# Selections, logits, one-hot transposes and scatters in another order on TensorE

## The chip, the core and the metric

The kernel runs on one core of a Trainium2 chip. The metric is the device time of one execution in microseconds (us); the median of several executions is compared. TensorE (PE) multiplies, VectorE (DVE) and ScalarE (ACT) copy and compute, GpSimd (POOL) helps, and SyncE (SP) issues most transfers. Engines run side by side and meet at semaphores; each works through its own instructions in the order in which they are written.

## The reference

```python
def _L0_gnn_ref(h, adj, Wq, bq, Wk, bk, Wv, bv, Wo, bo):   # masked attention, 8 heads
    ...
    scores = jnp.einsum('bhqd,bhkd->bhqk', q, k) * scale
    attn = jax.nn.softmax(jnp.where(mask, -jnp.inf, scores), axis=-1)
    ...
def _L0_ffn_ref(x, controller, f1, f2):                     # 64 expert slots, groups of t=16 tokens
    cont_logits = jnp.einsum('bgtd,des->bgtes', grouped, controller) + tie
    cont_perm = (cont_logits == jnp.max(cont_logits, axis=-3, keepdims=True)).astype(x.dtype)
    intermediate = jnp.einsum('bgtd,desf->bgtesf', grouped, f1)
    inner = jax.nn.relu(jnp.einsum('bgtesf,bgtes->bgesf', intermediate, cont_perm))
    inter2 = jnp.einsum('bgesf,esfd->bgesd', inner, f2)
    result = jnp.einsum('bgesd,bgtes->bgtd', inter2, cont_perm)
x = x + _L0_gnn_ref(_layernorm(x), ...)
x = x + _L0_ffn_ref(_layernorm(x), ...)
```

x is 32 x 256 x 256 in float32. In each group of 16 tokens every one of the 64 expert slots picks the token with the highest logit; the pick is a one-hot row. The second half of the kernel, which the change touches, selects those tokens, runs the experts on them and adds the results back to the tokens' rows.

## The kernel before

The 8192 token rows are 64 tiles of 128. The attention goes over 32 batches and fills the first two thirds of the span. The expert part goes over 4 chunks (c) of 16 tiles; a chunk is 4 units (u) of 4 tiles, and n = 4c + u counts the units from 0 to 15. After the four units of a chunk comes `experts(c)`.

What TensorE does in a unit (L909 to L931), each with the engine that takes the result:

- `unit_transpose(n + 2)` (L700) transposes the normalised tokens of the unit after next into banks 0 and 1; ScalarE copies them (`save_h2T`, L971).
- `select(n, t)` for t = 0 to 3 (L798) multiplies tokens by one-hots. A selection has two halves: the first goes to a bank pair that VectorE copies, the second to one that ScalarE copies (`copy_selected`, L284). The halves of t = 0 to 3 rotate over bank pairs 4, 6 and 0, so a half waits for the copy of the half three before it (L807 to L815): the second half of the fourth selection waits for VectorE's copy of the third.
- `one_hot_transpose(n + 1)` (L721) transposes the next unit's one-hots into bank 2; ScalarE copies them to `permR` (`save_one_hot`, L977).
- `logits(n + 2)` (L708) also writes bank 2, so it waits for that copy (`perm_saved`). On VectorE follow `tied_logits` (L1300), `group_maximum` (L1307) and `one_hot` (L1312).
- `scatter(c - 1, s)` (L895), two of them in each of the last three units of chunks 1 to 3, adds back the results of the chunk before: pair s is tiles 2s and 2s + 1, both into bank 3, and VectorE adds the bank to the tokens (`finish`, L1444). A scatter waits for the finish before it and, half by half, for its tile's results to have landed in SBUF (`gathered`, L902). Pairs 6 and 7 stand in `experts(c)` (L942).

The results of the experts go through HBM, since they are made by expert and needed by group. During `experts(c)` SyncE writes 16 blocks to `scratch` (`move`, L433). Then it gathers the 16 tiles, each in two halves (`gather`, L441), into a ring of 5 slots: tiles 0 to 4 follow each other as soon as the blocks are written, tile i from 5 on waits until tile i - 5 was scattered (L444). SyncE issues in order: first halves of tiles 0 to 3, then the second half of tile 0, of tile 1, and so on (L464 to L472).

In chunk 0 there are no scatters. There VectorE also does small steps of a reciprocal square root (`late_root_steps`, L1440) in unit 0 from t = 2 on, in units 1 and 2 and at the start of unit 3. In unit 0 it finishes the last attention batch as well. Units 14 and 15 have no unit transpose and no logits; unit 15 has no one-hot transpose.

Of the kernel before, what the change touches and what calls it, by code (L numbers as in the profile page):

```python
# [23 lines left out]
def gnn_moe_kernel(nc, x, adj, Wq, bq, Wk, bk, Wv, bv, Wo, bo, controller, f1, f2, out):  # L24
    B, N, D = x.shape
# [10 lines left out]
    CT = 16  # L36
    CHUNKS = TILES // CT
    UT = 4
    UNITS = CT // UT
# [9 lines left out]
    AHEAD = 2  # L49
# [24 lines left out]
    with ExitStack() as ctx:  # L74
# [88 lines left out]
        bank = [banks[:, i, :] for i in range(8)]  # L163
# [43 lines left out]
        res_done = sem("res_done")  # L207
# [380 lines left out]
        def _(pe):  # L588
# [101 lines left out]
            def o_project(b, last=False):  # L690
                pe.wait_ge(onorm_done, b + 1)
                if not last:
                    pe.wait_ge(q_saved, b + 3)
                for t in range(QT):
                    for g in range(G):
                        done = nc.tensor.matmul(M[1][:, t * D:t * D + D], OT[:, g, t * P:t * P + P], WT[:, 3, g, :],  # L696
                                                start=(g == 0), stop=(g == G - 1))
                done.then_inc(wo_ready, 1)
# [9 lines left out]
            def logits(n, into=bank[2]):  # L708

                pe.wait_ge(h2T_saved, n + 1)  # L710
                if n > 0:
                    pe.wait_ge(perm_saved, n)
                for k in range(KT):
                    for half in range(2):
                        r = slice(64 * half, 64 * half + 64)
                        own = h2T[:, k, :].rearrange("p (c two t) -> p c two t", two=2, t=T)[:, :, half, :]
                        last = nc.tensor.matmul(into[r, 0:UT * P // 2], ctl[:, k, :], own,  # L717
                                                start=(k == 0), stop=(k == KT - 1))
                last.then_inc(log_ready, 1)

            def one_hot_transpose(n, into=bank[2]):  # L721
                pe.wait_ge(perm_done, n + 1)
                for t in range(UT):
                    last = nc.tensor.transpose(into[:, t * P:t * P + P],
                                               permT[region(n)][:, t * P:t * P + P], ident[:, :])
                last.then_inc(pbt_ready, 1)
# [71 lines left out]
            def select(n, t):  # L798
                tile = n * UT + t
                if t == 0:  # L800
                    pe.wait_ge(perm_saved, n + 1)
                if tile == 0:
                    pe.wait_ge(perm_done, AHEAD)
                if t == 0 and n > 0 and n % UNITS == 0:
                    pe.wait_ge(st_dve, n // UNITS * QUADS)
                    pe.wait_ge(st_act, n // UNITS * QUADS)
                for hf in range(2):  # L807
                    if t == 0 and n > 0:
                        pe.wait_ge((sel_dve, sel_act)[hf], tile)
                    elif (t, hf) == (1, 0) and n + AHEAD < CHUNKS * UNITS:  # L810
                        pe.wait_ge(h2T_saved, n + AHEAD + 1)
                    elif (t, hf) == (1, 0):
                        pe.wait_ge(sel_act, tile - 2)
                    elif t > 0:
                        pe.wait_ge((sel_act, sel_dve)[hf], tile - 1 + hf)  # L815
                    for k in range(KT):
                        for j in (2 * hf, 2 * hf + 1):
                            r = slice(32 * j, 32 * j + 32)
                            last = nc.tensor.matmul(bank[pair_of(t, hf) + j % 2][:, k * P:k * P + P], h2[n % NORMS][r, t, k * P:k * P + P],  # L819
                                                    permR[r, n % 2, t * P:t * P + P], start=True, stop=True)  # L820
                    last.then_inc((sel_low, sel_ready)[hf], 1)
# [73 lines left out]
            def scatter(c, s):  # L895

                n = c * (CT // 2) + s
                if n > 0:
                    pe.wait_ge(fin_done, n)
                for tt in range(2):  # L900
                    tile = 2 * s + tt
                    pe.wait_ge(gathered[tile_slot(c, tile)], arrived(c, tile))  # L902
                    for j in range(4):
                        last = nc.tensor.matmul(bank[3][32 * j:32 * j + 32, tt * D:tt * D + D],  # L904
                                                chosen(c * CT + tile, j), XR[:, tile_slot(c, tile), j, :],
                                                start=True, stop=True)
                    last.then_inc(sc_ready, 1)

            def unit(c, u):  # L909

                n = c * UNITS + u
                ahead = n + AHEAD < CHUNKS * UNITS
                pairs = scatters(u) if c > 0 else ()
                if ahead:
                    if n > 0:
                        pe.wait_ge(sel_act, n * UT - 1)
                    unit_transpose(n + AHEAD)
                select(n, 0)
                if n + 1 < CHUNKS * UNITS:
                    one_hot_transpose(n + 1)  # L920
                if n == 0:
                    o_project(B - 1, True)
                select(n, 1)
                if ahead:
                    logits(n + AHEAD)
                select(n, 2)
                if pairs:
                    scatter(c - 1, pairs[0])
                select(n, 3)
                if pairs:  # L930
                    scatter(c - 1, pairs[1])  # L931

            def experts(c):
                pe.wait_ge(sel_dve, (c + 1) * CT)
                pe.wait_ge(sel_act, (c + 1) * CT)
                if c == 0:
                    pe.wait_ge(ffn_in, 16 * 2)
                expand(c, 0)
                for w in range(TWOS):
                    if w + 1 < TWOS:  # L940
                        expand(c, w + 1)
                    if c > 0 and w < len(LATE):  # L942
                        scatter(c - 1, LATE[w])
                    contract(c, w)

# [12 lines left out]
        def _(act):  # L958
# [18 lines left out]
            def save_one_hot(n, src=bank[2]):  # L977
                act.wait_ge(pbt_ready, n + 1)
                nc.scalar.copy(permR[:, n % 2, :], src[:, :]).then_inc(perm_saved, 1)
# [115 lines left out]
            def save_selected(c, u, t):  # L1095
                act.wait_ge(sel_ready, c * CT + u * UT + t + 1)
                copy_selected(nc.scalar.copy, c, u * UT + t, 1).then_inc(sel_act, 1)

            def unit(c, u):
                n = c * UNITS + u  # L1100
                ahead = n + AHEAD < CHUNKS * UNITS
                if ahead:
                    save_h2T(n + AHEAD)
                save_selected(c, u, 0)
                if n + 1 < CHUNKS * UNITS:
                    save_one_hot(n + 1)
                save_selected(c, u, 1)
                save_selected(c, u, 2)
                save_selected(c, u, 3)

            def experts(c):
# [25 lines left out]
        def _(dve):  # L1137
# [298 lines left out]
            def save_selected(c, u, t):  # L1436
                dve.wait_ge(sel_low, c * CT + u * UT + t + 1)
                copy_selected(nc.vector.tensor_copy, c, u * UT + t, 0).then_inc(sel_dve, 1)

            def late_root_steps(c, u, t):  # L1440
                if c == 0 and 2 <= u * UT + t < ROOT_STEPS + 2:
                    roots_step(u * UT + t - 2, slice((B - 4) * QT, TILES), late_root)
# [15 lines left out]
            def unit(c, u):  # L1458
                n = c * UNITS + u
                ahead = n + AHEAD < CHUNKS * UNITS  # L1460
                pairs = scatters(u) if c > 0 else ()
                save_selected(c, u, 0)
                late_root_steps(c, u, 0)
                save_selected(c, u, 1)
                if n == 0:
                    last_result()
                late_root_steps(c, u, 1)
                if ahead:
                    tied_logits(n + AHEAD)
                save_selected(c, u, 2)  # L1470
                late_root_steps(c, u, 2)
                if ahead:
                    group_maximum()
                if pairs:
                    finish(c - 1, pairs[0])
                save_selected(c, u, 3)
                late_root_steps(c, u, 3)
                if pairs:
                    finish(c - 1, pairs[1])
                if ahead:  # L1480
                    one_hot(n + AHEAD)
# [57 lines left out]
```

## Time and profile before

| | |
|---|---|
| median of 3 runs | 752.02 us (750.18 to 753.73) |
| the profiled execution, its own time | 753.89 us |
| its span, first to last instruction | 752.0 us |
| mean granted TensorE clock | 0.988 |
| PE busy, share of the span | 711.2 us, 95% |
| DVE, ACT, POOL busy | 79%, 72%, 24% |
| chain that ended last: PE | 86% |
| chain: waits on the gathers (DMA stage<-scratch) | 2% |

The page has the busy time of each engine, the span in 40 slices, the chain of work that ended last followed back from the end, and the costliest groups. In a row of the timeline stand the start and the duration in us, the engine, the line of the kernel, the operation, the tile written and the tile read, the shape and the count of merged instructions; in square brackets the idle time of that engine before it, and what ended it. PEld is the loading of TensorE's weights, which overlaps the multiplication; a matmul shows here as two instructions, a transpose as one. SPq is SyncE issuing a transfer. The granted clock is given as a share of the full 2.4 GHz, so that 0.5 is 1.2 GHz.

### The profile page before, as it was taken

How to read it: one execution, taken by the hardware profiler on the slowest of the kernel's cores; microseconds unless marked ns; L12 is line 12 of the kernel's file. 1: busy time of each engine (PE TensorE's matmuls, PEld its weight loads, DVE VectorE, ACT ScalarE, POOL GpSimd, SP SyncE). 2: the span in 40 equal slices, each digit the busy share in tenths (PEclk: the TensorE clock that was granted, in tenths of full speed). 3: DMA queues.
4: the chain of work that ended last, by engine and by line, in shares of the span. 5: the costliest groups of instructions: out<-in, count | busy, mean ns of one | idle time of the engine just before them, and what ended most of it. 6: DMA issues, size and time to landing. Idle time of an engine off the chain costs nothing.

```text
span 752.0 us, 22953 instructions
## 1 busy us (share of the span) xinstructions
PE 711.2 (95%) x7420; PEld 575.8 (77%) x7420; DVE 595.7 (79%) x2418; ACT 544.2 (72%) x1606; POOL 181.2 (24%) x375
## 2 busy tenths in 40 slices
PE   8899999999999999999999999989879979878888
PEld 7788888888888888888888888866656656655666
DVE  6698898898988988989889888986656756656566
ACT  4788989898889898988899889874445344344243
POOL 2130321302303213023032130646705506400000
PEclk9999999999999999999999999998999999999999
DMA  6776787677867877778678767746099798798943
GB/s 179 185 184 143 185 196 163 166 187 166 193 147 177 194 164 167 185 168 193 150 174 194 166 144 157 158 87 218 3 394 300 261 388 276 265 383 271 342 164 104
DMA packets 110742, 149.24 MB, mean 198 GB/s; under 512 B 14784, under 2 KB 75712, under 8 KB 110432
## 3 DMA queue, kind: packets, MB, share of 16 engines
q1 hardware_dynamic: 107904, 146.26, 72.0%
q10 hardware_dynamic: 2592, 1.71, 1.0%
q8 instruction: 37, 0.61, 0.3%
q0 software_dynamic: 192, 0.52, 0.2%
q14 instruction: 17, 0.14, 0.1%
HBM read 39.39 MB, written 33.55 MB: 97 GB/s over the span
## 4 chain that ended last, share of the span: by engine, by line
PE 86%; DVE 6%; issue 3%; DMA 2%; ACT 2%; SPq 1%; POOL 0%; DVEq 0%; POOLq 0%
PE bank L672 15%; PE bank L624 15%; PE bank L659 8%; PE bank L685 8%; PE bank L696 8%; PE bank L646 7%; PE bank L819 5%; PE bank L861 3%; DVE stage L1503 3%; PE bank L904 3%; DMA stage<-scratch 2%; PE bank L717 2%; PE bank L877 2%; PE bank L617 2%; PE bank L704 2%
## 5 line engine op out<-in xcount | busy, mean ns | idle before, releaser
L1026 ACT ACTIVATE Ps<-Ps,nmax 128x256 f32<-128x256 f32 x512 | 254.6, 501 | 19.8 <-DVE nmax L1246 19.8
L1246 DVE CUSTOM_DVE_ANT_0 Ps<-bank,masks 128x256 f32<-128x256 f32 x512 | 193.0, 421 | 28.6 <-issue 28.4
L672 PE MATMUL bank<-ident,Ps 128*128 128x128 f32 x1024 | 134.8, 274 | 2.5 <-ACT Ps L1026 1.8
L672 PEld LDWEIGHTS bank<-ident,Ps 128*128 128x128 f32 x1024 | 114.8, 141 | 11.9 <-issue 3.3
L624 PE MATMUL bank<-hT,WT 128*128 128x256 f32 x512 | 121.1, 380 | 0.3 <-ACT hT L983 0.3
L624 PEld LDWEIGHTS bank<-hT,WT 128*128 128x128 f32 x512 | 92.4, 190 | 10.7 <-ACT Vs L999 0.7
L549 POOL TENSOR_SCALAR h<-X,mv,roots 128x256 f32<-128x256 f32 x64 | 79.6, 1255 | 78.7 <-PE bank L819 76.5
L1026 ACT ACTIVATION_READ_ACCUMULATOR Ps<-Ps,nmax 128x1 f32 x512 | 97.4, 190 | 0.0
L659 PE MATMUL bank<-stack 128*128 128x256 f32 x512 | 91.5, 311 | 0.6 <-DMA stack<-parts 0.6
L1257 DVE COPY PTs<-bank 128x512 f32<-128x512 f32 x128 | 86.7, 677 | 0.2
L659 PEld LDWEIGHTS bank<-stack 128*128 128x128 f32 x512 | 71.7, 189 | 17.3 <-issue 13.1
L1035 ACT COPY PTs<-bank 128x512 f32<-128x512 f32 x128 | 73.5, 574 | 11.5 <-PE bank L672 11.5
L508 POOL TENSOR_TENSOR spread<-rsum,nans 128x128 f32<-128x128 f32 x32 | 12.9, 405 | 232.9 <-DVE rsum L1263 232.9
L1009 ACT ACTIVATE parts<-bank,few 128x256 fp32r<-128x256 f32 x128 | 53.0, 464 | 21.3 <-PE bank L624 21.3
L685 PE MATMUL bank<-PTs,Vs 128*32 128x256 f32 x1024 | 61.9, 382 | 0.8 <-DVE PTs L1257 0.8
L696 PE MATMUL bank<-WT,OT 128*128 128x256 f32 x256 | 62.3, 386 | 0.2
L646 PE MATMUL bank<-WT,hT 128*128 128x256 f32 x256 | 62.1, 387 | 0.0
L1120 ACT COPY stage<-bank 128x512 f32<-128x512 f32 x48 | 25.8, 589 | 49.6 <-PE bank L861 49.6
L819 PE MATMUL bank<-permR,h 32*128 32x128 f32 x1024 | 55.5, 303 | 5.5 <-DVE XS L292 3.2
L819 PEld LDWEIGHTS bank<-permR,h 32*128 32x128 f32 x1024 | 43.0, 192 | 23.0 <-issue 10.3
L1232 DVE SCALAR_TENSOR_TENSOR parts<-bank,few,parts 128x256 fp32r<-128x256 f32 x128 | 55.8, 479 | 1.9 <-ACT parts L1009 1.9
L292 ACT COPY XS<-bank 128x512 f32<-128x512 f32 x48 | 28.3, 589 | 32.7 <-PE bank L819 31.8
(107 smaller groups left out, 1052.9 us busy)
## 6 DMA issues: line engine op xcount, KB each, us to landing
stack<-parts SPq DMA_DIRECT2D x506, 128.0 KB, 2.5
scratch<-stage SPq DMA_DIRECT2D x48, 512.0 KB, 4.3
stage<-scratch SPq DMA_DIRECT2D x96, 256.0 KB, 4.4
X<-in_x SPq DMA_DIRECT2D x32, 256.0 KB, 2.9
out<-X SPq DMA_DIRECT2D x32, 256.0 KB, 3.7
rbc<-turned SPq DMA_DIRECT2D x126, 64.0 KB, 2.1
f1s<-in_L_ffn_f SPq DMA_DIRECT2D x1, 2048.0 KB, 8.5
f2s<-in_L_ffn_f SPq DMA_DIRECT2D x1, 2048.0 KB, 14.2
```

The source lines that it names most:

```text
L549: last = nc.gpsimd.tensor_scalar(h2[n % NORMS][:, t, :], xtile(tile), mv2[:, tile, 0:1], roots[:, 1, tile:tile + 1], ALU.subtract, ALU.mult)
L624: last = nc.tensor.matmul(m[:, g * N:g * N + N], WT[:, w, k, g * P:g * P + P], hT[:, k, :], start=(k == 0), stop=(k == KT - 1))
L646: last = nc.tensor.matmul(M[0][:, t * D:t * D + D], hT[:, k, t * P:t * P + P], WT[:, 2, k, :], start=(k == 0), stop=(k == KT - 1))
L659: last = nc.tensor.matmul(s_bank(n)[:, h * N:h * N + N], stack[:, par, j, 0, g * N + t * P:g * N + t * P + P], stack[:, par, j, 1, g * N:g ...
L672: last = nc.tensor.transpose(PTb[h % 2][:, k * N + t * P:k * N + t * P + P], Ps[:, pr % 2, t, h % 2, k * P:k * P + P], ident[:, :])
L685: last = nc.tensor.matmul(into[32 * j:32 * j + 32, g * N:g * N + N], Vs[:, par, k, h * DH:h * DH + DH], PTs[:, slot_of(h), k * N:k * N + N ...
L696: done = nc.tensor.matmul(M[1][:, t * D:t * D + D], OT[:, g, t * P:t * P + P], WT[:, 3, g, :], start=(g == 0), stop=(g == G - 1))
L819: last = nc.tensor.matmul(bank[pair_of(t, hf) + j % 2][:, k * P:k * P + P], h2[n % NORMS][r, t, k * P:k * P + P], permR[r, n % 2, t * P:t ...
L1026: last = nc.scalar.activation(Ps[:, pr % 2, t, h, :], Ps[:, pr % 2, t, h, :], ACT.Exp, bias=nmax[:, pr % 2, t, h:h + 1], scale=-1.0, accum ...
L1035: nc.scalar.copy(PTs[:, h, :], PTb[h % 2][:, :]).then_inc(pt_act, 1)
L1246: last = nc.vector.tensor_tensor_reduce(out=Ps[:, pr % 2, t, h, :], in0=s_bank(n)[:, h * N:h * N + N], in1=masks[:, t, :], scale=1.0, scal ...
L1257: nc.vector.tensor_copy(PTs[:, h, :], PTb[h % 2][:, :]).then_inc(pt_dve, 1)
```

## The change

Within the units the same instructions are issued in another order, and some waits go with them. On TensorE, for units 1 to 14, before and after:

```
before: transpose, select 0, one-hot transpose, select 1, logits, select 2, scatter, select 3, scatter
after:  transpose, select 0, scatter, select 1, logits, select 2, one-hot transpose, select 3, scatter
```

The one-hot transpose of those units goes to bank 3, where the scatters also write, and not to bank 2. It therefore waits for the finish of the first scatter, and the second scatter waits for ScalarE's copy of the one-hots. The logits no longer wait for that copy, but for VectorE's one-hot of the unit before. Unit 0 keeps its order on TensorE. ScalarE's copy of the one-hots moves behind its copy of the third selection. On VectorE the first finish moves behind the copy of the first selection, and the copy of the third selection moves behind the reduction of the logits (`group_maximum`) and, in chunk 0, behind the root step.

```diff
--- before.py
+++ after.py
@@ -708,7 +708,9 @@
             def logits(n, into=bank[2]):
 
                 pe.wait_ge(h2T_saved, n + 1)
-                if n > 0:
+                if n > AHEAD:
+                    pe.wait_ge(perm_done, n)
+                elif n > 0:
                     pe.wait_ge(perm_saved, n)
                 for k in range(KT):
                     for half in range(2):
@@ -916,18 +918,24 @@
                         pe.wait_ge(sel_act, n * UT - 1)
                     unit_transpose(n + AHEAD)
                 select(n, 0)
-                if n + 1 < CHUNKS * UNITS:
-                    one_hot_transpose(n + 1)
                 if n == 0:
+                    one_hot_transpose(1)
                     o_project(B - 1, True)
+                if pairs:
+                    scatter(c - 1, pairs[0])
                 select(n, 1)
                 if ahead:
                     logits(n + AHEAD)
                 select(n, 2)
-                if pairs:
-                    scatter(c - 1, pairs[0])
+                if 0 < n < CHUNKS * UNITS - 1:
+                    if c > 0:
+                        pe.wait_ge(fin_done, (c - 1) * (CT // 2) + (pairs[0] + 1 if pairs else 0))
+                    elif n == 1:
+                        pe.wait_ge(res_done, B)
+                    one_hot_transpose(n + 1, bank[3])
                 select(n, 3)
                 if pairs:
+                    pe.wait_ge(perm_saved, min(n + 2, CHUNKS * UNITS))
                     scatter(c - 1, pairs[1])
 
             def experts(c):
@@ -940,6 +948,8 @@
                     if w + 1 < TWOS:
                         expand(c, w + 1)
                     if c > 0 and w < len(LATE):
+                        if w == 0:
+                            pe.wait_ge(perm_saved, min((c + 1) * UNITS + 1, CHUNKS * UNITS))
                         scatter(c - 1, LATE[w])
                     contract(c, w)
 
@@ -1102,10 +1112,12 @@
                 if ahead:
                     save_h2T(n + AHEAD)
                 save_selected(c, u, 0)
-                if n + 1 < CHUNKS * UNITS:
-                    save_one_hot(n + 1)
+                if n == 0:
+                    save_one_hot(1)
                 save_selected(c, u, 1)
                 save_selected(c, u, 2)
+                if 0 < n < CHUNKS * UNITS - 1:
+                    save_one_hot(n + 1, bank[3])
                 save_selected(c, u, 3)
 
             def experts(c):
@@ -1461,18 +1473,18 @@
                 pairs = scatters(u) if c > 0 else ()
                 save_selected(c, u, 0)
                 late_root_steps(c, u, 0)
+                if pairs:
+                    finish(c - 1, pairs[0])
                 save_selected(c, u, 1)
                 if n == 0:
                     last_result()
                 late_root_steps(c, u, 1)
                 if ahead:
                     tied_logits(n + AHEAD)
-                save_selected(c, u, 2)
                 late_root_steps(c, u, 2)
                 if ahead:
                     group_maximum()
-                if pairs:
-                    finish(c - 1, pairs[0])
+                save_selected(c, u, 2)
                 save_selected(c, u, 3)
                 late_root_steps(c, u, 3)
                 if pairs:
```

## Rows read from the trace of the kernel before

**Rows 1.** Timeline, TensorE (PE) and its weight loads (PEld), unit 6.

```profile
576.75 1.09 PE L704 MATMUL bank<-ident,h 128*128 128x128 f32 x8
577.77 0.74 PE L819 MATMUL bank<-permR,h 32*128 32x128 f32 x16
578.44 0.66 PE L724 MATMUL bank<-ident,permT 128*128 128x128 f32 x4
579.03 0.77 PEld L819 LDWEIGHTS bank<-permR,h 32*128 32x128 f32 x16 [0.17 <-ACT h2T L974]
580.04 0.66 PEld L717 LDWEIGHTS bank<-h2T,ctl 128*64 128x64 f32 x8 [0.25 <-issue]
581.76 1.07 PE L904 MATMUL bank<-stage,permT 128*32 128x256 f32 x16
583.64 0.59 PEld L904 LDWEIGHTS bank<-stage,permT 128*32 128x32 f32 x16 [0.33 <-DVE X L1449]
584.64 1.09 PE L704 MATMUL bank<-ident,h 128*128 128x128 f32 x8
```

**Rows 2.** Timeline, VectorE (DVE), the same unit.

```profile
581.20 0.42 DVE L1303 TENSOR_TENSOR LT<-bank,tie 128x256 f32<-128x256 f32 x1 [0.71 <-PE bank L717]
581.85 0.69 DVE L292 COPY XS<-bank 128x512 f32<-128x512 f32 x1 [0.23 <-PE bank L819]
582.46 0.41 DVE L1310 TENSOR_REDUCE gmax<-LT 128x16 f32<-128x256 f32 x1
```

**Rows 3.** Timeline, PEld, unit 2: second half of the fourth selection.

```profile
531.03 0.52 PEld L819 LDWEIGHTS bank<-permR,h 32*128 32x128 f32 x8 [0.54 <-DVE XS L292]
```

**Rows 4.** Timeline, PE: the first transposes of units 5, 9 and 13.

```profile
568.86 1.09 PE L704 MATMUL bank<-ident,h 128*128 128x128 f32 x8
622.81 1.09 PE L704 MATMUL bank<-ident,h 128*128 128x128 f32 x8
677.59 1.09 PE L704 MATMUL bank<-ident,h 128*128 128x128 f32 x8
```

**Rows 5.** Gather of tile 1, second half, three chunks, and landing; last, all 96.

```profile
568.92 0.62 SPq L446 DMA_DIRECT2D stage<-scratch  x1
DMA to landing us min/median/max: 4.4/4.4/4.4
622.98 0.62 SPq L446 DMA_DIRECT2D stage<-scratch  x1
DMA to landing us min/median/max: 4.8/4.8/4.8
677.85 0.62 SPq L446 DMA_DIRECT2D stage<-scratch  x1
DMA to landing us min/median/max: 3.8/3.8/3.8
DMA to landing us min/median/max: 3.0/4.4/6.3
```

**Rows 6.** Timeline, PEld: last scatter half behind units 7 and 11.

```profile
598.51 0.16 PEld L904 LDWEIGHTS bank<-stage,permT 128*32 128x32 f32 x8 [1.11 <-DMA stage<-scratch]
653.28 0.16 PEld L904 LDWEIGHTS bank<-stage,permT 128*32 128x32 f32 x8 [2.03 <-DMA stage<-scratch]
```

**Rows 7.** Timeline, units 14 and 15: one-hot transpose, scatter, last scatter half.

```profile
687.13 0.42 PEld L724 LDWEIGHTS bank<-ident,permT 128*128 128x128 f32 x4 [1.09 <-DVE permT L1322]
690.06 1.94 PE L904 MATMUL bank<-stage,permT 128*32 128x256 f32 x16
700.22 0.16 PEld L904 LDWEIGHTS bank<-stage,permT 128*32 128x32 f32 x8 [1.33 <-DMA stage<-scratch]
```

**Rows 8.** Stretches: us, busy us (count) of PE, PEld, DVE, ACT, POOL, clock, DMA share, GB/s.

```profile
515.50:522.40 6.90, 6.90 (x56) 5.37 (x58) 3.31 (x8) 3.32 (x6) 5.36 (x4) 0.51 0.55 174
651.10:653.90 2.80, 1.25 (x28) 0.36 (x20) 0.83 (x2) 0.29 (x1) 0.00 (x0) 1.00 0.83 324
689.60:693.10 3.50, 3.50 (x40) 1.79 (x37) 0.86 (x2) 0.62 (x1) 0.00 (x0) 0.51 0.78 245
```

## What I expect of the change

> **What bounds the kernel now.** I read the page first: TensorE is busy 95% of the span and holds 86% of the chain that ended last, the gathers' transfers 2%. The change touches only the expert part, so I went on with the timeline there, unit by unit, and then asked for every wait in one unit who ended it. [rows 1] are unit 6, which stands for the five units of its kind (5, 6, 7 in chunk 1, 9 to 11 in chunk 2 and 13 in chunk 3 are spaced alike). It takes 584.64 - 576.75 = 7.89 us. From start to start the transpose takes 1.02, a selection 0.67, the one-hot transpose 0.59 and a scatter 1.00; 581.76 less 580.08, where the logits begin behind the load at 580.04, leaves 1.68 for logits and a selection, so 1.01 for the logits. The sum 1.02 + 4 x 0.67 + 0.59 + 1.01 + 2.00 is 7.30. So 0.59 us of a unit are waits: about 0.38 at the second selection and the logits behind it (h2T, VectorE's first copy, ScalarE's copy of the one-hots), and 0.21 before the second scatter, which waits for the first finish. That is all that another order can win in such a unit, 8% of it.
>
> **A unit of the new order.** I lay the durations of [rows 1] end to end, with the unit's start at 0. Selection 0 starts at 1.02, the first scatter at 1.69, selection 1 at 2.69 (its copies are long done), the logits at 3.36, selection 2 at 4.37, the one-hot transpose at 5.04, selection 3 at 5.63. The second half of selection 3 waits for VectorE's copy of selection 2. On VectorE the tied logits start 1.12 behind the logits [rows 1, 2], so at 4.5; the group maximum needs their result and starts some 0.46 later, and the copy stands behind it by a further 0.33 (0.41 of work, overlapped a little), so it starts at 5.3. Ahead of the group maximum it would start 0.76 behind its selection (581.85 less 581.76 - 0.67), at 5.13. It takes 0.69 and ends at 5.98, and its signal reaches TensorE at 6.03. A half selection that has to wait takes 0.64 to the next instruction: in unit 2 it started at 531.03 and the transpose behind it at 531.68 [rows 3]. The second scatter then starts at 6.03 + 0.64 = 6.67, with the one-hots copied by ScalarE at about 6.4, and the unit ends at 7.67. The three waits are gone, a new one of 0.37 is there: **0.22 us gained in a unit**, not 0.59. The finish at the end of the unit and the one-hot behind it end 1.6 into the next unit on VectorE, before its first copy is due at 1.78: no cost.
>
> **Units without a scatter.** In unit 2 of chunk 0 the last selection already waits 0.54 for the same copy [rows 3]. The group maximum, and in units 0 to 2 a root step of 0.2, now stand in front of that copy. I take 0.6 for unit 0, where VectorE was late already, 0 for unit 1, where TensorE ran at half clock for most of it [rows 8], 0.2 for unit 2, 0 for unit 3. Units 4, 8 and 12 lose 0.15 each in the same way. Chunk 0 together: +0.8.
>
> **The step that costs: the first scatter of units 5, 9 and 13.** It moves from 5.0 us into the unit to 1.7. It needs tiles 0 and 1 in SBUF, and these come at a time that TensorE's order does not set: SyncE gathers them as soon as the last block is written. The second half of tile 1 was issued at 568.92, 622.98 and 677.85 and landed 4.4, 4.8 and 3.8 later, so at 573.3, 627.8 and 681.65 [rows 5]. The units began at 568.86, 622.81 and 677.59 [rows 4]; in the old order the scatter stood right behind the landing. In the new one, with the 0.15 from the unit before, its second half would be due 0.15 + 1.69 + 0.5 into the unit: 571.2, 625.15, 679.93. **TensorE waits 2.1, 2.65 and 1.7 us**, with nothing else in its queue to do, and selections 1 to 3 and the logits, which used to fill that time, stand behind. This is 6.45 us, the largest term. The later tiles are no trouble: tile 5 is freed earlier than before, and each scatter of units 6, 7, 10 and 11 comes a whole unit behind the one that frees its slot.
>
> **What comes back at the end of the chunk.** Behind the units the last scatters wait for tile 15. The idle time was 1.11 and 2.03 [rows 6], of which 0.3 is the usual spacing between two halves: 0.8 and 1.72. The gathers of tiles 13 and 14 hang on the first scatter of units 7 and 11, which is now 3.3 us earlier in its unit, so tile 15 no longer queues behind them. I count all of it as won. ScalarE's last copy comes 0.1 later for the experts.
>
> Chunk 1: 0.15 - 0.22 + 2.1 - 2 x 0.22 + 0.1 - 0.8 = +0.9. Chunk 2: 0.15 - 0.22 + 2.65 - 0.44 + 0.1 - 1.72 = +0.5.
>
> Chunk 3: 0.15 - 0.22 + 1.7 = +1.6 up to unit 14. Unit 14 was slow: 1.09 waiting for the one-hots of unit 15 [rows 7] and a scatter of 1.94 at half clock, 8.6 in all. In the new order that transpose comes after selection 2, when the one-hots are long there. Laid end to end I get 6.7: waits of 0.2 (finish of unit 13), some 0.9 for VectorE's copies, which are late behind the one-hot of unit 15, and 0.3 for ScalarE's copy of the one-hots. That is -1.9. Unit 15 waited 1.33 - 0.3 for tile 11 [rows 7], which now comes earlier; I count -0.9. Chunk 3: -1.1.
>
> Sum without the clock: 0.8 + 0.9 + 0.5 - 1.1 = **+1.1 us**.
>
> **The clock.** Both stretches of [rows 8] at 0.51 lie behind gaps of TensorE: of 1.1 us before the one-hot transpose of unit 15 [rows 7], and of VectorE's late copies in unit 0. A stretch at half level costs: the scatter at 690.06 took 1.94 in place of 1.07, and I take 1.2 us for the 3.5 us stretch as a whole, since some waits shrink in it. The new gaps are longer than those, with one scatter half between them, so I expect a fall behind each: 3 x 1.2 = 3.6. Against it speaks the stretch from 651.1 to 653.9, where TensorE was busy 1.25 of 2.80 us and the clock stayed at full level [rows 8]. Bounds: 0 if none falls, and 3 x 2.9 if each lasts as long as the 6.9 us at 515.5.
>
> The sum is +4.7 us. Against the profiled execution that is 753.89 + 4.7 = 758.6; this run was 1.9 above the median of 752.02, so the median should go to **756.7**.
>
> The Trainium skill, DMA: Bandwidth & Descriptors, "Rules for kernel authors", asks that a transfer be issued early and its semaphore be waited on late; the change moves the wait earlier and leaves the issue where it is, and the trace agrees that there is no room. The same page, "Anatomy of one DMA", gives about 2.0 us plus the bytes at 436 GB/s, an estimate of 2.6 us for 256 KB; the rows show 3.8 to 4.8. By the page the three waits would be 1.2 us shorter each than with landings of 3.8 and the time below 750, and no row of a gather is as short.
>
> **The rivals.**
> 1. *The clock holds.* The gaps are as computed, but none brings the half level, as at 651. Then 752.02 + 1.1 = 753.1, no change that can be told from none.
> 2. *The gathers land sooner, the change pays.* The shortest of the 96 landings was 3.0 us [rows 5]. With it for tile 1 the waits are 0.7, 0.85 and 0.9, 4.0 less than the forecast has, and too short to bring the clock down: 752.02 + 1.1 - 4.0 = 749.1, and with a little luck elsewhere under 748.3. For it: TensorE reads nothing of the DMA in that time. Against it: the blocks' writes are still in the queues when the gathers start, in all three chunks alike. It decides where landings fall under 3.3.
> 3. *The half level lasts twice as long* behind each gap, as at 515.5: 752.02 + 1.1 + 8.7 = 761.8.
>
> **How the numbers follow.** About 0.5% (3.8 us) is what a measurement of this kernel can tell from no change. Forecast 756.7: 0.48. Clock holds, 753.1: 0.30. Sooner landings, 749.1: 0.09. Longer falls, 761.8: 0.13. Cases between them, one or two falls in place of three, lie between 753.1 and 756.7. The range 750.0 to 762.0 takes in the forecast and the first and third rival, with the 1.8 us by which runs of one kernel differ. Over 755.8 lie most of the forecast's case and all of the third: slower 0.54. Same: the clock that holds, a fourth of the forecast's case and half of the sooner landings, 0.41. Faster 0.05.
>
> **What the profile of the changed kernel would show.** In units 5, 9 and 13 a wait of TensorE on the gathers of about 2 us before and within the first scatter, with landings as before. Units 6, 7, 10 and 11 at about 7.67 us. The waits on DMA behind units 7 and 11 gone. The one-hot wait of unit 14 gone. Stretches of granted clock at half level in units 5, 9 and 13. The forecast is wrong if tile 1 lands within 3.3 us of its issue, if the clock stays up, or if units 6 and 7 come to 7.3, which would mean that VectorE's copy of the third selection does not wait for the group maximum.

## The result and the profile after

The changed kernel takes 758.0 us in the median of 20 runs (751.65 to 763.33), the kernel before 752.92 us in 20 runs beside it (749.47 to 757.86). The ratio is 1.0061, 95% interval 1.0042 to 1.0080: slower by 4.6 us, where 4.7 was forecast (756.7 from the median of three runs, 752.02). One of the 20, at 763.33 and over 1.5% above the fastest, counts as slow and is left out of the ratio. Beside the last experiments the same instructions came to 1.0056 (1.0033 to 1.0079).

The profiled execution took 761.25 us, its span 759.3. The page first: the granted clock in 40 slices, and the chain that ended last by engine, where the transfers (DMA) rose from 2% to 5%.

```profile
PEclk9999999999999999999999999997999999999999
...
PE 85%; DVE 5%; DMA 5%; issue 3%; ACT 2%; SPq 0%; POOL 0%; DVEq 0%; POOLq 0%
```

Then the stretches, cut at the starts of the units: unit 1, 5, 6, 8, 9, 10, 13, 14 and 15 of the changed kernel. The columns are those of [rows 8]: length, then busy time and count of PE, PEld, DVE, ACT and POOL, then granted clock, share of the transfer engines, GB/s.

```profile
517.03:526.98 9.95, 9.95 (x86) 7.31 (x84) 3.81 (x10) 4.00 (x7) 5.03 (x4) 0.53 0.21 66
...
569.35:581.30 11.95, 9.52 (x119) 5.79 (x117) 5.47 (x10) 4.42 (x8) 5.92 (x5) 0.86 0.76 248
581.30:588.97 7.67, 7.67 (x120) 5.15 (x117) 5.63 (x10) 3.83 (x7) 4.83 (x5) 1.00 0.75 234
...
619.54:627.17 7.63, 7.39 (x87) 5.79 (x85) 4.39 (x8) 4.36 (x8) 0.00 (x0) 0.84 0.95 333
627.17:636.13 8.96, 7.95 (x118) 5.08 (x116) 5.41 (x10) 4.42 (x8) 5.92 (x5) 1.00 0.95 304
636.13:643.80 7.67, 7.67 (x120) 5.15 (x116) 5.63 (x10) 3.83 (x7) 4.83 (x5) 1.00 0.82 261
...
682.01:693.51 11.50, 9.39 (x118) 5.78 (x117) 5.38 (x10) 4.61 (x8) 0.00 (x0) 0.85 0.81 256
693.51:700.17 6.66, 5.94 (x104) 3.91 (x101) 4.71 (x8) 3.08 (x5) 0.00 (x0) 1.00 0.76 238
700.17:705.69 5.52, 5.02 (x96) 3.32 (x96) 3.92 (x6) 2.51 (x4) 0.00 (x0) 1.00 1.00 307
```

Units 5, 9 and 13, all 7.9 us before, now take 11.95, 8.96 and 11.50. Units 6 and 10 take 7.67, as forecast to the hundredth, and units 14 and 15 take 6.66 and 5.52 in place of 8.6 and 6.4. Set beside the profile before, stretch by stretch, the 7.3 us by which the two spans differ are:

| stretch | forecast without clock | measured |
|---|---|---|
| units 0 to 3 | +0.8 | +2.0, of it 1.2 in unit 1 at half clock |
| experts of chunk 0 | 0 | -1.6, no half-clock stretch there this time |
| units 4, 8, 12 | +0.15 each | +0.1, +0.8, +0.6, the last two begun at half clock |
| units 5, 9, 13 | +1.9, +2.4, +1.5 | +4.1, +1.1, +3.6 |
| units 6, 7, 10, 11 | -0.2, -0.1 | -0.2, -0.1, -0.2, -0.1 |
| experts of chunks 1 and 2, with the late scatters | -0.8, -1.7 | -0.7, -1.3 |
| unit 14 | -1.9 | -1.95 |
| unit 15 | -0.9 | -0.85 |
| behind unit 15 | 0 | +2.1 |

The timeline of unit 5, loads of TensorE, shows the term that was thought the largest:

```profile
570.37 0.55 PEld L821 LDWEIGHTS bank<-permR,h 32*128 32x128 f32 x16 [0.17 <-issue]
573.49 0.16 PEld L906 LDWEIGHTS bank<-stage,permT 128*32 128x32 f32 x8 [2.57 <-DMA stage<-scratch]
574.18 0.19 PEld L906 LDWEIGHTS bank<-stage,permT 128*32 128x32 f32 x8 [0.53 <-DMA stage<-scratch]
575.18 0.96 PEld L821 LDWEIGHTS bank<-permR,h 32*128 32x128 f32 x16 [0.81 <-issue]
576.36 0.29 PEld L719 LDWEIGHTS bank<-h2T,ctl 128*64 128x64 f32 x4 [0.22 <-issue]
```

Selection 0 at 570.37, then nothing for 2.57 us until tile 0 has landed, half a scatter, another wait for tile 1, and selection 1 at 575.18, 5.8 us into the unit in place of 2.69. And the work behind runs slowly: from 575.18 to 576.36 a selection takes 1.18 in place of 0.67. The clock had fallen, from 574.2 to 577.7 it stood at 0.51:

```profile
574.20:577.70 3.50, 3.50 (x32) 1.90 (x32) 1.38 (x2) 0.59 (x1) 0.43 (x1) 0.51 0.89 288
516.20:526.40 10.20, 10.20 (x80) 7.45 (x80) 4.61 (x12) 3.48 (x7) 5.03 (x4) 0.50 0.29 93
686.90:690.30 3.40, 3.40 (x32) 1.81 (x28) 1.38 (x2) 0.63 (x1) 0.00 (x0) 0.50 0.98 307
```

Unit 6 is the new order without a wait on transfers. TensorE, VectorE's group maximum and its copy of the third selection, and the fourth selection that waits for the copy:

```profile
581.30 0.86 PEld L704 LDWEIGHTS bank<-ident,h 128*128 128x128 f32 x8 [0.41 <-ACT XS L292]
...
586.25 0.42 DVE L1322 TENSOR_REDUCE gmax<-LT 128x16 f32<-128x256 f32 x1
...
586.59 0.68 DVE L292 COPY XS<-bank 128x512 f32<-128x512 f32 x1
586.93 0.91 PEld L821 LDWEIGHTS bank<-permR,h 32*128 32x128 f32 x16 [0.17 <-issue]
...
587.97 0.59 PEld L906 LDWEIGHTS bank<-stage,permT 128*32 128x32 f32 x16
588.97 0.86 PEld L704 LDWEIGHTS bank<-ident,h 128*128 128x128 f32 x8 [0.41 <-ACT XS L292]
```

The copy starts 5.29 us into the unit, the loads of the fourth selection stretch to 0.91 against 0.55, and the second scatter starts at 6.67: the numbers of the forecast. And of the late waits of [rows 6] this is left:

```profile
601.57 0.22 PEld L906 LDWEIGHTS bank<-stage,permT 128*32 128x32 f32 x8 [0.21 <-DMA stage<-scratch]
...
656.38 0.24 PEld L906 LDWEIGHTS bank<-stage,permT 128*32 128x32 f32 x8 [0.19 <-DMA stage<-scratch]
```

### The profile page after: what moved, and what is told of

Its sections match the earlier page's. It is cut to its first block, busy times and chain, and to the rows that moved or that the text cites. A ratio compares the mean times of both kernels' runs of the same rounds, so it can differ in the third digit from the quotient of the medians.

```text
span 759.3 us, 22965 instructions
## 1 busy us (share of the span) xinstructions
PE 718.5 (95%) x7420; PEld 581.0 (77%) x7420; DVE 597.0 (79%) x2418; ACT 544.6 (72%) x1606; POOL 180.1 (24%) x375
## 4 chain that ended last, share of the span: by engine, by line
PE 85%; DVE 5%; DMA 5%; issue 3%; ACT 2%; SPq 0%; POOL 0%; DVEq 0%; POOLq 0%
PE bank L672 15%; PE bank L624 14%; PE bank L659 8%; PE bank L685 8%; PE bank L696 8%; PE bank L646 7%; PE bank L821 5%; PE bank L863 4%; DVE stage L1515 3%; PE bank L906 3%; DMA stage<-scratch 3%; PE bank L879 2%; PE bank L719 2%; DMA scratch<-stage 2%; PE bank L617 2%
## 5 line engine op out<-in xcount | busy, mean ns | idle before, releaser
L821 PEld LDWEIGHTS bank<-permR,h 32*128 32x128 f32 x1024 | 46.2, 198 | 24.3 <-issue 12.0
L821 PE MATMUL bank<-permR,h 32*128 32x128 f32 x1024 | 59.1, 310 | 5.2 <-DVE XS L292 2.1
```

## The experiments

My theory was that the change wins in most units, about what was forecast, and loses more than that in units 5, 9 and 13, to the gathers and to the clock behind them. The rival was that the loss lies in the other units: in VectorE's order, or in bank 3, which the one-hots now share with the scatters. All kernels below are cut from the change with one set of units, NEW, that gets the new order on TensorE, ScalarE and VectorE; the others keep the old one.

| kernel | ratio to before | 95% interval |
|---|---|---|
| the change | 1.0061 | 1.0042 to 1.0080 |
| units 5, 9, 13 old | 0.9957 | 0.9929 to 0.9985 |
| units 5, 9, 13 alone new | 1.0128 | 1.0087 to 1.0170 |
| copy ahead of the group maximum | 1.0006 | 0.9976 to 1.0036 |
| filler matmuls | 1.0019 | 0.9988 to 1.0051 |
| two early gathers, not four | 1.0025 | 1.0003 to 1.0046 |
| units 14 and 15 alone new | 0.9975 | 0.9945 to 1.0005 |
| units 6, 7, 10, 11, 14, 15 new, copy first | 0.9905 | 0.9869 to 0.9941 |
| all but 5, 9, 13 new, copy first | 0.9927 | 0.9902 to 0.9951 |
| the change, again | 1.0056 | 1.0033 to 1.0079 |
| filler matmuls, again | 1.0008 | 0.9979 to 1.0037 |
| copy first and filler | 0.9982 | 0.9958 to 1.0005 |
| units 6, 7, 10, 11 alone new, copy first | 0.9942 | 0.9912 to 0.9972 |

### Units 5, 9 and 13 in the old order

```diff
-    NEW = set(range(1, 16))
+    NEW = set(range(1, 16)) - {5, 9, 13}
```

> Units 5, 9 and 13 in the order of before on all three engines, all other units as in the change. My theory (the change loses what TensorE waits for the gathers of tiles 0 and 1, and the clock that falls with it): no wait on the gathers in these three units, which come back to 7.9 us each from 11.95, 8.96 and 11.5; what stays is chunk 0 (+2.0), units 4, 8, 12 (+0.15 each), units 6, 7, 10, 11 (-0.2 each), the waits behind units 7 and 11 (-0.7 and -1.3) and units 14 and 15 (-2.8). Together about -3 us against the kernel before: ratio 0.996, between 0.993 and 0.999. Rival (the loss lies in the other units, in VectorE's order or in bank 3): ratio stays at 1.004 or above.

Measured: 0.9957, as forecast from the theory and far from the rival. Unit 5 takes 7.90 us again. Its first scatter stands at 574.20, five us into the unit, behind its work and without a wait:

```profile
573.53 0.55 PEld L823 LDWEIGHTS bank<-permR,h 32*128 32x128 f32 x16 [0.39 <-issue]
574.20 0.59 PEld L908 LDWEIGHTS bank<-stage,permT 128*32 128x32 f32 x16
```

So three of the fifteen reordered units turn a kernel that is 0.4% faster than the one before into one that is 0.6% slower: 7.8 us between the two ratios.

### Units 5, 9 and 13 alone in the new order

```diff
-    NEW = set(range(1, 16))
+    NEW = {5, 9, 13}
```

> The kernel before, with units 5, 9 and 13 alone in the new order. My theory: these three units carry the whole loss, and none of the gains of the others is there to pay for it: +1.9, +2.4, +1.5 us for the waits and 1 to 1.5 for each clock fall, so +6 to +9 us, ratio 1.008 to 1.012. Rival (the loss comes from the other units): ratio within 1.002 of 1.

Measured: 1.0128, just above the range expected (to 1.012). Units 5 and 9 take 11.56 and 11.52 us, and the clock falls behind the wait in all three units in this execution. Behind units 7 and 11, which are in the old order here, the late waits are all there, 1.13 and 2.52 us, where the kernel before had 1.11 and 2.03.

```profile
566.62 0.16 PEld L908 LDWEIGHTS bank<-stage,permT 128*32 128x32 f32 x8 [2.27 <-DMA stage<-scratch]
...
597.70 0.16 PEld L908 LDWEIGHTS bank<-stage,permT 128*32 128x32 f32 x8 [1.13 <-DMA stage<-scratch]
...
656.64 0.16 PEld L908 LDWEIGHTS bank<-stage,permT 128*32 128x32 f32 x8 [2.52 <-DMA stage<-scratch]
```

A delay of TensorE in unit 5 gives the gathers of tiles 13 to 15 nothing: each still hangs on a scatter five tiles earlier, which was delayed with everything else.

### VectorE's copy ahead of the group maximum

In the kernel a set of unit numbers decides this; it holds all units here, so the edit comes to:

```diff
+                save_selected(c, u, 2)
                 late_root_steps(c, u, 2)
                 if ahead:
                     group_maximum()
-                save_selected(c, u, 2)
                 save_selected(c, u, 3)
```

> The change, but VectorE copies the third selection ahead of the root step and the group maximum, as before. My theory (the second half of the fourth selection waits for that copy, which is late behind the group maximum): units 6, 7, 10 and 11 take 7.50 in place of 7.67, units 0 and 2 come back to 9.4 and 6.5, units 4, 8 and 12 win 0.15; together some 2 us less than the change, ratio to before 1.003. Rival (the fourth selection waits for something else): unit 6 stays at 7.67 and the ratio at 1.006.

Measured: 1.0006. Unit 6 takes 7.53 us, against 7.50 expected and 7.67 in the change, so the mechanism is shown:

```profile
582.86 0.69 DVE L294 COPY XS<-bank 128x512 f32<-128x512 f32 x1 [0.22 <-PE bank L823]
...
583.35 0.77 PEld L823 LDWEIGHTS bank<-permR,h 32*128 32x128 f32 x16 [0.17 <-issue]
583.46 0.41 DVE L1328 TENSOR_REDUCE gmax<-LT 128x16 f32<-128x256 f32 x1
```

The copy starts 0.76 behind its selection and the loads of the fourth selection shrink from 0.91 to 0.77. The gain, about 4 us, is larger than the 2 that the units explain. In this execution the half-clock stretch in chunk 0 was 3.4 us, where it was 10.2 in the change. But it was 10.2 again in a later kernel with the copy first (all units but 5, 9 and 13 new), so VectorE's order does not set it. Over all executions the mean granted clock was 0.989 here and 0.987 in the change, which is some 4 us less at half level. So the part of the gain beyond the units lies, by this, in the clock; why it fell less here is not shown. With the filler of the next section in place, where the clock falls rarely, the copy first was worth 2.0 us (1.0008 against 0.9982), what the units explain.

### Filler matmuls in the wait

Written without the set NEW, which holds every unit with a scatter here:

```diff
                 if pairs:
+                    if u == 1:
+                        pe.wait_ge(perm_done, n + 2)
+                        for _ in range(8):
+                            nc.tensor.matmul(bank[2][:, 0:P], ident[:, :], ident[:, :], start=True, stop=True)
                     scatter(c - 1, pairs[0])
```

> The change, with 8 more matmuls of the identity into bank 2 in front of the first scatter of units 5, 9 and 13, so that TensorE works through most of the wait for tile 0. Landings and the end of the wait stay where they are. My theory (a part of the loss, 1 to 1.5 us for each stretch at half clock, comes from the clock, not from the wait): the granted clock stays at full level in units 5 and 13, each of which shortens by 1 to 1.5 us; ratio 1.003. Rival (the clock falls for other reasons, or what it costs is hidden by the waits): half level in units 5 and 13 as before, ratio 1.006 or above.

Measured: 1.0019. The intervals of this and of the change overlap, so the pair ran once more side by side, with a third kernel that has both this and the copy first.

> The change itself, the same instructions, beside the next two on one chip, so that the filler can be compared with it directly. Ratio to before 1.006 by all theories, between 1.003 and 1.009.

> The change with the 8 filler matmuls, once more. My theory (1 to 1.5 us of each of the three waits is the clock that falls behind it): 3 to 4 us less than the change beside it, ratio to before 1.002. Rival (the first difference was the spread of the runs, the filler does nothing): the same ratio as the change beside it, 1.006.

> The filler and VectorE's copy of the third selection ahead of the group maximum, together. If the two gains are separate (3.5 us of clock, 0.14 us in each of the 13 units with logits behind it and more in chunk 0): 6 us less than the change, ratio to before 0.998. If the copy-first kernel won by falling less often and not by its shorter units, the two overlap and the ratio is that of the better one, 1.001.

Measured: 1.0056, 1.0008 and 0.9982. The filler, which computes nothing of use, is worth 3.6 us by these ratios, between the 3 and 4 forecast. The noise is not small beside it: the means of the twelve times of each are 3.1 us apart, with a 95% interval of 1.0 to 5.1. With the copy first the kernel is 5.6 us faster than the change, as expected of two separate gains (6 us) and less than the 7.7 that the first two measured gains would give together (3.6 and 4.1). In the first of the filler kernels unit 5 looks so:

```profile
565.55:575.20 9.65, 9.65 (x134) 6.99 (x132) 5.41 (x10) 4.42 (x8) 5.91 (x5) 1.00 0.95 303
```

```profile
567.24 1.86 PEld L931 LDWEIGHTS bank<-ident 128*128 128x128 f32 x16
...
569.22 0.16 PEld L908 LDWEIGHTS bank<-stage,permT 128*32 128x32 f32 x8
...
569.58 0.23 PEld L908 LDWEIGHTS bank<-stage,permT 128*32 128x32 f32 x8 [0.20 <-DMA stage<-scratch]
```

TensorE multiplies for 2 us where it waited, the clock stays at 1.00, and the unit takes 9.65: 7.67 and 2.0 for the wait. With the clock down it was 11.95. Of these 2.3 us the clock is 1.5, read from the rows of the two units 5 (the second half of the scatter took 0.36 more than here, selection 1 0.51, the logits 0.62); the other 0.8 is tile 1, which landed 4.8 us behind its issue there and 4.0 here.

The second profile of the change is a control without filler. The same instructions wait in unit 5, and the clock does not fall; in unit 9 it does:

```profile
572.71 0.16 PEld L908 LDWEIGHTS bank<-stage,permT 128*32 128x32 f32 x8 [1.75 <-DMA stage<-scratch]
573.43 0.16 PEld L908 LDWEIGHTS bank<-stage,permT 128*32 128x32 f32 x8 [0.56 <-DMA stage<-scratch]
```

```profile
569.38:578.98 9.60, 7.95 (x118) 5.06 (x117) 5.41 (x10) 4.42 (x8) 5.91 (x5) 1.00 0.94 299
623.77:636.19 12.42, 9.22 (x118) 5.85 (x117) 5.48 (x10) 4.42 (x8) 5.91 (x5) 0.86 0.77 243
```

Unit 5 takes 9.60 with an idle TensorE and 9.65 with a busy one, so the filler neither shortens nor lengthens the wait; what it can save is the fall behind it, and that does not come each time. In the five profiled kernels that wait in units 5, 9 and 13 without filler the clock fell behind 9 of the 15 waits, in the three with filler behind none of 9. The length of the wait alone does not tell which: it fell behind 2.25 us of idle time (two early gathers, unit 9) and held behind 3.52 (copy first, unit 9).

How much of the 3.6 us comes from there is not settled, for the profiles show a second difference. Stretch 516.2 to 526.4, in chunk 0, in the change and in the filler kernel of this pair:

```profile
516.20:526.40 10.20, 10.20 (x80) 7.51 (x80) 4.62 (x12) 3.41 (x6) 4.89 (x4) 0.51 0.29 92
```

```profile
516.20:526.40 10.20, 9.21 (x132) 7.18 (x130) 7.12 (x19) 5.98 (x11) 8.16 (x7) 1.00 0.29 93
```

Units 0 and 1 take 19.96 us in the one and 16.31 in the other, though the filler stands only in units 5, 9 and 13 and TensorE waits the same 2.32 us in unit 0 of both. All three profiled filler kernels lack this stretch, and all six others with the new order in chunk 0 have it, one of them 3.4 us long. The mean clocks of all executions point the same way: from 0.988 in the change to 0.994 with the filler is some 10 us less at half level, but from 0.987 in the change to 0.990 with units 5, 9 and 13 in the old order, without those waits, only some 6. Whether the filler has to do with chunk 0, or that is chance, no run here decides.

### Two early gathers in place of four

```diff
-            EARLY = 4
+            EARLY = 2
```

> The change, but SyncE gathers the first halves of only two tiles (not four) ahead of the second halves of tiles 0 and 1. The second half of tile 1 is still issued when the last block is written, but two gathers of 256 KB fewer are ahead of it in the queues. My theory (TensorE waits for what the transfer engines still have to move, at some 300 GB/s): the landing comes 1 to 1.7 us earlier, the waits in units 5, 9 and 13 shrink to about 1 us each, the clock falls less often; ratio 1.001, between 0.998 and 1.004. Rival (a landing is a fixed 4 to 5 us behind its issue, whatever is queued): waits of 2 us as before and ratio 1.006.

Measured: 1.0025, interval up to 1.0046, where the change's begins at 1.0042. The second half of tile 1 in chunk 1, issue and time to landing, in the change (with the gather issued just before it) and in this kernel:

```profile
L446 SPq DMA_DIRECT2D stage<-scratch x2: 580/600/619, 568.6 to 569.3; - x2
...
DMA to landing us min/median/max: 4.8/4.8/4.9
```

```profile
L448 SPq DMA_DIRECT2D stage<-scratch x1: 1139/1139/1139, 568.4 to 568.4; - x1
...
DMA to landing us min/median/max: 3.9/3.9/3.9
```

It landed 0.9 us sooner, less than the 1 to 1.7 expected. But the filler kernel and the second run of the change, with four early gathers, had 4.0 too. And the waits did not shrink to 1 us: TensorE was idle 2.2, 2.25 and 2.0 us before and within the first scatters of units 5, 9 and 13, against 3.1, 1.65 and 2.7 in the change and 2.3, 3.8 and 2.2 in its second profile. So the time is nearer to the theory than to the rival, the profile does not bear out its mechanism, and how much of a landing is what stands ahead in the queues stays open.

### Units 14 and 15 alone

```diff
-    NEW = set(range(1, 16))
+    NEW = {14, 15}
```

> The kernel before, with units 14 and 15 alone in the new order. My theory (the one-hot transpose of unit 15 waits no more for VectorE, and tile 11 is there in time): unit 14 goes from 8.6 to about 6.9 us, unit 15 from 6.4 to 5.6, no clock fall at 689; ratio 0.997, between 0.995 and 0.999. Rival (the scatters of chunk 3 wait for landings anyway, so what units 14 and 15 save is waited for behind them): ratio 1.000.

Measured: 0.9975, between 0.9945 and 1.0005: near the forecast value, though the interval just reaches 1. Unit 14 takes 7.15 us and unit 15 5.75, and the clock stays up there. The one-hot transpose of unit 15 now comes without a wait, but ahead of it TensorE waits for tile 3, in the second scatter of unit 13, and for tile 5, in the first of unit 14:

```profile
682.90 0.16 PEld L908 LDWEIGHTS bank<-stage,permT 128*32 128x32 f32 x8 [1.40 <-DMA stage<-scratch]
...
685.57 0.16 PEld L908 LDWEIGHTS bank<-stage,permT 128*32 128x32 f32 x8 [1.06 <-DMA stage<-scratch]
...
688.29 0.42 PEld L728 LDWEIGHTS bank<-ident,permT 128*128 128x128 f32 x4
```

The first of the two stands in unit 13, ahead of anything that was changed in this kernel, so it is the landing of this execution and not the order. The second does take back a part of what unit 14 saves. In the change itself these waits are absent: unit 13 took 11.50 us, and the gathers had the time. In its second profile unit 13 took 9.46, and the wait for tile 5 was back, 0.86.

### Units 6, 7, 10 and 11 alone, and two larger sets

The second of the three kernels here has NEW = {6, 7, 10, 11, 14, 15}, the third set(range(1, 16)) - {5, 9, 13}; in all three VectorE copies first.

```diff
-    NEW = set(range(1, 16))
+    NEW = {6, 7, 10, 11}
```

> The kernel before, with units 6, 7, 10 and 11 alone in the new order and VectorE's copy of the third selection kept ahead of the group maximum. My theory: 4 x 0.36 us from the units themselves and 0.8 and 1.7 from the waits for tile 15 behind units 7 and 11: -3.9 us, ratio 0.995. Rival (the waits for tile 15 only move with the earlier scatters and stay as long): -1.4 us, ratio 0.998.

> New order only in units 6, 7, 10, 11, 14 and 15, with VectorE's copy of the third selection ahead of the group maximum; all others as before. From the unit times of the runs so far: units 6, 7, 10 and 11 win 0.36 each, the waits behind units 7 and 11 win 0.8 to 1.5 each, units 14 and 15 win 2.8: -6 us, ratio 0.992. Rival (the gains are taken back by clock falls elsewhere): ratio 0.996 or above.

> As the kernel with units 5, 9 and 13 in the old order, with VectorE's copy of the third selection ahead of the group maximum everywhere. What it has over the run before it in this list is the new order in chunk 0 and in units 4, 8 and 12, where the shown unit times with the copy first were 9.0, 7.6 and 6.3 in place of 9.4, 8.8 and 6.5. If these hold, ratio 0.990; if they were a matter of where the clock fell in one execution, the ratio is that of the run before, 0.992.

Measured: 0.9942, 0.9905 and 0.9927. The first says that four units and the late waits behind them are worth 4.4 us, near the 3.9 expected and not the 1.4 of the rival: the waits for tile 15 do not only move. Its last scatters behind units 7 and 11 start without one:

```profile
592.00 0.67 PEld L908 LDWEIGHTS bank<-stage,permT 128*32 128x32 f32 x16
...
644.84 0.67 PEld L908 LDWEIGHTS bank<-stage,permT 128*32 128x32 f32 x16
```

The second has units 14 and 15 besides and the lowest ratio, 746.8 us in the median of seven runs against 752.7: 7.2 us or 1% faster than the kernel before by the ratio, and 1.5% faster than the change. The third was to be faster still and is not. The intervals of all three overlap, so which of them is the fastest is not shown. The new order in chunk 0 and in units 4, 8 and 12 is worth nothing that shows, as the rival there had it.

## Why the prediction was right, point by point

**The unit of the new order.** Laid end to end from the durations before, it gave 7.67 us, and that is what units 6 and 10 measured. Units 7 and 11 are not of the same kind, as the forecast took them to be: they took 7.57 before and 7.49 and 7.50 after, so 0.07 is won there and not 0.22. The one new wait, for VectorE's copy behind the group maximum, was at its place, and without it the unit came to 7.53.

**The first scatter of units 5, 9 and 13.** Right in mechanism and in order of size. Unit 5: 2.1 us forecast for the wait; 2.0 and 1.9 measured in the two executions whose clock stayed up there, and 2.8 in the first profile of the change (11.95 less 7.67 and 1.5 for the clock), where tile 1 landed later. What was not seen is that the wait depends on what happened before. In chunk 2 TensorE came 0.8 us later to unit 9, because the clock stood at half level at the start of unit 8, the gathers did not, and of 2.65 us of wait 1.3 were left (8.96 less 7.67).

**What comes back.** The late waits behind units 7 and 11: -0.8 and -1.7 forecast, -0.7 and -1.3 measured. Units 14 and 15: -1.9 and -0.9 forecast, -1.95 and -0.85 measured. The two kernels that have only these parts in the new order agree with it as time, 0.9942 and 0.9975, the second with an interval that reaches 1.

**The clock.** Three falls at 1.2 us, 3.6 together, were forecast, one behind each wait. A fall cost 1.5 in unit 5, and they did not come each time: in the first profile behind the waits of units 5 and 13 and not behind that of unit 9, in the second behind that of unit 9 alone. The clock also stood low where none was forecast: in the first profile at the starts of units 8 and 12, in chunk 0 longer than before, and once behind unit 15. The mean clock of all executions, 0.987 in the change and 0.993 in the kernel before, means some 20 us at half level against some 10: three stretches of 3.4 us more, as many as forecast. But by the kernel with units 5, 9 and 13 in the old order, at 0.990, only about half of them go with the waits of those units, an estimate of 2.5 us of time in place of 3.6. The rival in which the clock holds is refuted by the stretches at 0.51 in units 5 and 13. That of the sooner landings fell with the landings of 4.8 and 4.5 us in the first two chunks. The rival of doubled falls was not seen behind the waits, but in chunk 0, where the stretch lasted 10.2 us. That short waits would leave the clock up, as the rival of sooner landings had it, rested on no row; the stretch at 689.6 lay behind a wait of 1.1.

**Chunk 0.** The step that was undersized: +0.8 forecast, +2.0 measured in this profile, all the excess in unit 1. I took 0 there because TensorE ran at half clock anyway; what I left out is that the half-clock stretch itself can become longer, 10.2 us here against 6.8. Of the nine profiled kernels with the new order in chunk 0 five had 10.2 us, one 3.4 and three none, and these three are the ones with filler; of the five with the old order one had 6.8, one 3.4 and three none. So the term may be partly one of chance, and whether the later end of unit 0 brings the long stretches is open.

**The total.** That 4.6 and 4.7 us agree to 0.1 is luck. The profiled executions differ by 7.3 us, and terms that the forecast did not have, -1.6 in the experts of chunk 0, +1.1 more than forecast in units 8 and 12 and +2.1 behind unit 15, go with where the clock happened to fall. What the runs bear out is the direction, the waits of about 2 us in units 5, 9 and 13 as the largest term, and the gains elsewhere that do not pay for them.

The Trainium skill's estimate of 2.6 us for 256 KB (DMA: Bandwidth & Descriptors, "Anatomy of one DMA") is worked out from a fit for transfers that GpSimd issues. These are issued by SyncE, and the second halves of tile 1 landed 3.8 to 5.3 us behind their issue with 16 blocks of 512 KB written just before. The Trainium skill's rule to issue a transfer early and wait on it late (the same page, "Rules for kernel authors") is what the change broke in three units; in units 6, 7, 10 and 11 the gathers are issued earlier along with the wait.

## What to carry to other kernels

Before moving a consumer of a transfer forward, ask what sets the arrival: if it is set by the consumer's own earlier work (a ring of slots, as in units 6 and 7), moving it forward brings the next arrival forward too; if it is set by something outside (here the last block written before unit 5), the consumer only waits, and all that stood between is pushed back. One order for all iterations of a loop hides this: choose it per iteration. And count a wait of TensorE by its length and by the clock that may fall behind it, which here took about 1.5 us more behind 9 of 15 such waits of some 2 us.

## What the runs showed of the hardware

A wait of TensorE for transfers, 2.57 us and after half a scatter 0.53, was followed by a granted clock of 0.51 for 3.5 us, which cost 1.5. The same instructions in another execution waited 1.75 and 0.56 us, and the clock stayed at 1.00. With eight matmuls of the identity in the place of the wait it stayed up in all nine units of three profiles, and the kernel was 3.6 us faster (3.1 by the means, 1.0 to 5.1), though not all of that is shown to come from there.

The length of the half-clock stretch in chunk 0 changed between executions with the same order of instructions there: none, 3.4 or 6.8 us in the old order, none, 3.4 or 10.2 in the new, once 10.2 and once none behind the same wait of 2.32 us. That is reason enough not to read 1 or 2 us from one profile.
